# Two more tiles of attention in three rounded terms, and the last of the ring's tiles summed by a transfer

## The reference, cut to what matters

```python
kv = context @ Wkv;  k, v = split(kv);  q = layernorm(x) @ Wq       # B=8, N=56, M=1500, D=128, 16 heads of 64
dots = einsum('bhnd,bhmd->bhnm', q, k) * 64 ** -0.5
dots = dots - (1 - mask)[:, None, :, None] * 1e6
out = einsum('bhnm,bhmd->bhnd', softmax(dots), v)                    # heads merged
x = x + out @ Wout + bout
h = gelu(einsum('etd,edf->etf', layernorm(x).reshape(8, T, D), w1) + b1)   # one expert for each batch, F=512
x = x + (einsum('etf,efd->etd', h, w2) + b2).reshape(x.shape)
```

## Time and profile before

| | |
|---|---|
| median of 3 runs | 373.58 us (373.33 to 374.76) |
| the profiled execution | 373.79 us, of it span 371.9 us from the first to the last instruction |
| TensorE clock granted | 0.998 of full speed over the span |
| TensorE, VectorE, ScalarE, GpSimd busy | 97%, 75%, 68%, 31% of the span |
| scores, line 444 | 576 matmuls of 448 columns |
| float32 tiles, line 484 | 248 records; split tiles, line 477: 192 |
| exponential, seed, ex_hi (ScalarE) | 917, 911, 937 ns each |
| ex_lo, addition, half copy of shift_row (VectorE) | 1088, 1090, 620 ns each |

### The profile page before, as it was taken

How to read it: one execution, slowest core, us unless ns; L and a number is a source line. 1 busy time by engine, 2 the same in 40 slices (tenths; PEclk the granted TensorE clock), 3 DMA queues, 4 the chain that set the end, 5 groups by cost and what they waited for, 6 DMA issues and landing times.

```text
span 371.9 us, 5778 instructions
## 1 busy us (share of the span) xinstructions
PE 361.5 (97%) x1713; PEld 277.4 (75%) x1713; DVE 278.7 (75%) x458; ACT 254.6 (68%) x335; POOL 114.8 (31%) x125
## 2 busy tenths in 40 slices
PE   7899999999999999999999999999999999999994
PEld 7667777777877877777777877777777877677754
DVE  5888667877787778978797669978697669454863
ACT  3456577697669566797769576797579476896621
POOL 1610573145313530145314430254314440022000
PEclk9999999999999999999999999999999999999999
DMA  7696369328942846339932854349933752338400
GB/s 238 215 187 179 62 118 208 88 84 151 202 112 75 158 81 152 84 95 235 235 99 82 148 99 132 84 114 234 227 87 95 136 99 49 119 71 153 74 2 6
DMA packets 30622, 47.10 MB, mean 127 GB/s; under 512 B 2011, under 2 KB 21371, under 8 KB 30608
## 3 DMA queue, kind: packets, MB, share of 16 engines
q0 software_dynamic: 9936, 27.40, 37.8%
q1 hardware_dynamic: 20672, 19.52, 17.7%
HBM read 24.59 MB, written 0.23 MB: 67 GB/s over the span
## 4 chain that ended last, share of the span: by engine, by line
PE 88%; DVE 7%; DMA 2%; issue 2%; ACT 1%; SPq 1%; DVEq 0%; ACTq 0%
PE ps_s L444 30%; PE ps_a L484 24%; PE ps_x L500 11%; PE ps_a L477 10%; PE ps_x L533 3%; PE ps_a L421 2%; DVE ex_sum L901 2%; DMA ctxt_raw<-in_ctx_t 2%; PE ps_x L553 2%; PE ps_x L562 1%; PE ps_x L458 1%; PE ps_x L530 1%; PE ps_x L509 1%; PE ps_x L510 1%; DVE chunk_max L920 1%
## 5 line engine op out<-in xcount | busy, mean ns | idle before, releaser
L920 DVE TENSOR_REDUCE chunk_max<-ps_x 128x1 f32<-128x500 f32 x168 | 110.8, 677 | 29.3 <-PE ps_x L500 26.4
L709 ACT ACTIVATE ex_all<-ps_s 125x896 f32<-125x896 f32 x95 | 87.1, 917 | 39.0 <-PE ps_s L444 37.9
L484 PE MATMUL ps_a<-ex_all,ctx_sb 125*128 125x448 f32 x248 | 109.8, 540 | 0.0
L727 ACT COPY ps_s<-shift_row 125x896 f32<-125x896 f32 x94 | 85.7, 911 | 15.1 <-DVE shift_row L1058 12.6
L500 PE MATMUL ps_x<-ctxt_hi,qk_hi 128*128 128x500 f32 x168 | 80.0, 478 | 1.7 <-DVE chunk_max L920 1.2
L1236 POOL DMA_DIRECT2D ex_all<-ex_all x48 | 42.2, 878 | 115.3 <-ACT ex_all L709 110.9
L444 PE MATMUL ps_s<-qk_hi,ctxt_hi 128*125 128x448 f32 x192 | 73.9, 466 | 0.0
L484 PEld LDWEIGHTS ps_a<-ex_all,ctx_sb 125*128 125x128 f32 x248 | 46.2, 189 | 18.9 <-issue 14.6
L444 PE MATMUL ps_s<-qk_hi,ctxt_lo 128*125 128x448 f32 x192 | 54.9, 367 | 0.0
L444 PE MATMUL ps_s<-qk_lo,ctxt_hi 128*125 128x448 f32 x192 | 54.7, 366 | 0.0
L444 PEld LDWEIGHTS ps_s<-qk_hi,ctxt_hi 128*125 128x125 f32 x192 | 35.7, 187 | 22.3 <-issue 20.7
(11 more groups left out here) (110 smaller groups left out, 382.1 us busy)
## 6 DMA issues: line engine op xcount, KB each, us to landing
ex_all<-ex_all POOLq DMA_DIRECT2D x48, 448.0 KB, 4.6
ctxt_raw<-in_ctx_t SPq DMA_DIRECT2D x8, 750.0 KB, 6.8
ctx_sb<-in_ctx SPq DMA_DIRECT2D x8, 750.0 KB
ctxt_hi<-in_ctx_t POOLq DMA_DIRECT2D x21, 250.0 KB, 3.4
...
```

The costliest lines, as they stand in the source:

```text
L484: mm = nc.tensor.matmul(ps_a[:, c, 0:CH], ctx_sb[0:MT, u, t, :], ex(t)[0:MT, c * CH:(c + 1) * CH], start=(slot == 0), stop=(slot == TM - 1))
L709: nc.scalar.activation(half(ex(t)[0:MT, :]), src, ACT.Exp, scale=SCALE).then_inc(ex_ready, 1)
L727: nc.scalar.copy(ps_s[0:MT, t % 2, :, 0:CH], half(shift_row[0:MT, b.parity, :])).then_inc(seeded, 1)
L920: nc.vector.tensor_reduce(chunk_max[:, k, t:t + 1], filled()[:, 0:MC], AX.X, ALU.max).then_inc(job_free, 1)
```

## The change

- Tiles 7 and 9 are split too: `SPLIT` is 2, 4, 6, 7, 8, 9, in the last batch without 9. The order of the products is 6, 7, 8, 9 instead of 7, 6, 9, 8. `ctx_hi` and `ctx_lo` are made in two parts, the part of tiles 7 to 9 at t = 11 (ScalarE) and t = 4 (GpSimd).
- Tile 9 is added by a transfer into tile 0, except in the last batch. The additions left are 1 + 10, 2, 0, 11: two at (11, 0), one at (11, 1), one at (0, 0) of the next batch. The exponential of the next tile 0 now waits for the third of them.
- The seed of the next batch's tile 0 is copied from `ps_x` itself by ScalarE, which then copies `ps_x` into `shift_row` too and frees both jobs (`first_seed`); VectorE's two copies are gone, except for batch 0's.
- `sum_hi` shares the memory of `shift_diag`.

```diff
@@ -115,11 +115,13 @@
...
-    SUM_PARTS = [9, 1, 10, 2, 11]
-    SUMS = len(SUM_PARTS)
-    SPLIT = [2, 4, 6, 8]
-    PV_ORDER = [0, 1, 2, 3, 5, 4, 7, 6, 9, 8, 10, 11]
-    SPLITS, CTX_HI_AT = len(SPLIT), 5
+    CHAIN_TILES = [[3, 6, 9], [4, 7], [5, 8]]
+    SUM_PARTS, LAST_SUM_PARTS = [1, 10, 2, 0, 11], [0, 9, 1, 10, 2, 11]
+    SUMS, LAST_SUMS = len(SUM_PARTS) - 1, len(LAST_SUM_PARTS) - 1
+    SPLIT = [2, 4, 6, 7, 8, 9]
+    PV_ORDER = [0, 1, 2, 3, 5, 4, 6, 7, 8, 9, 10, 11]
+    SPLITS, CTX_HI_AT = len(SPLIT), (5, 11)
+    CTX_PARTS = [slice(0, 3), slice(3, 6)]
@@ -143,8 +145,8 @@
...
-    ADD_AT = {(10, 2): (0,), (11, 0): (1, 2)}
-    ADD_LATE = (3, 4)
+    ADD_AT = {(11, 0): (0, 1), (11, 1): (2,)}
+    ADD_LATE = (3,)
@@ -183,7 +185,7 @@
...
-        sum_hi = sb("sum_hi", [P, Q], F32R)
+        sum_hi = shift_diag[:, :, :].rearrange("p t q -> p (t q)")
@@ -268,22 +271,32 @@
...
+        def split(b):
+
+            return SPLIT[:-1] if b.off == B - 1 else SPLIT
+
+        def buffer_free(n):
+
+            return read_by(SPLIT[n - 2]) if n >= 2 else read_by(SPLIT[SPLITS - 2 + n]) - TM
...
         def summed(t):
-            return 1 + (SUM_PARTS.index(t) if t else 0)
+            return max(SUM_PARTS.index(t), 1)
...
         def added_by_dma(eng, b, t):
-            adds = LAST_DMA // CHAINS
-            eng.wait_ge(ex_added[t % CHAINS], b.at(16 * adds, 16 * (t // CHAINS)))
+            c, n = t % CHAINS, CHAIN_TILES[t % CHAINS].index(t)
+            eng.wait_ge(ex_added[c], b.at(16 * len(CHAIN_TILES[c]), 16 * (n + 1)))
@@ -564,7 +577,8 @@
...
             def shift_jobs():
-                for c in range(2):
+                for _ in range(2):
+                    c = jobs.n % 2
                     shift_rows(job()[:, 0:CH], P, c, start=True).then_inc(job_ready, 1)
@@ -712,19 +726,25 @@
...
-                if n >= 2:
-                    act.wait_ge(pv_done, b.at(TM, read_by(SPLIT[n - 2])))
+                wait(act, pv_done, b.at(TM, buffer_free(n)))
                 nc.scalar.copy(ex_hi[0:MT, n % 2, :], ex(t)[0:MT, :]).then_inc(ex_hi_ready, 1)
...
+            def first_seed(b):
+
+                act.wait_ge(job_ready, jobs.value())
+                act.wait_ge(ex_ready, b.at(TM, -1))
+                nc.scalar.copy(ps_s[0:MT, 0, :, 0:CH], ps_x[0:MT, :, 0:CH]).then_inc(seeded, 1)
+                nc.scalar.copy(half(shift_row[:, b.parity, :]), ps_x[:, :, 0:CH]).then_inc(job_free, 2)
@@ -806,15 +826,18 @@
                     elif prepare:
                         if t + 2 == TM:
                             jobs.n = FIRST_JOBS if first else jobs.n + 2
+                            first_seed(b.later(1))
+                        else:
                             act.wait_ge(job_free, jobs.value())
-                        seed(b.later(1), t + 2 - TM)
+                            seed(b.later(1), 1)
...
+                        for part in range(2):
+                            ctx_high_part(b, part)
+                    if t in CTX_HI_AT and prepare:
+                        ctx_high_part(b.later(1), CTX_HI_AT.index(t))
+                    if t in split(b):
                         ex_high_part(b, SPLIT.index(t))
                     if pair is not None and t == GELU_AT[0]:
                         gelu_sigmoid(pair)
@@ -888,21 +911,20 @@
...
-                t = SUM_PARTS[n]
+                parts, by_dma = (LAST_SUM_PARTS, LAST_DMA) if b.off == B - 1 else (SUM_PARTS, TM)
                 dst = ex_sum[0:MT, b.parity, :]
-                left = ex(0)[0:MT, :] if n == 0 else dst
-                if n == 0:
-                    added_by_dma(dve, b, LAST_DMA - CHAINS + 1)
-                if t < CHAINS:
-                    added_by_dma(dve, b, LAST_DMA - CHAINS + 1 + t)
-                else:
-                    dve.wait_ge(ex_ready, b.at(TM, t + 1))
+                left = ex(parts[0])[0:MT, :] if n == 0 else dst
+                for t in parts[0:2] if n == 0 else parts[n + 1:n + 2]:
+                    if t < CHAINS:
+                        added_by_dma(dve, b, max(s for s in CHAIN_TILES[t] if s <= by_dma))
+                    else:
+                        dve.wait_ge(ex_ready, b.at(TM, t + 1))
                 wait(dve, ex_summed, b.at(SUMS, n))
                 nc.vector.tensor_tensor(dst, left, ex(t)[0:MT, :], ALU.add).then_inc(ex_summed, 1)
@@ -1068,7 +1090,7 @@
...
                     if prepare and at == SHIFT_AT:
-                        shift_copies(b.later(1))
+                        jobs.n += 2
@@ -1113,7 +1135,7 @@
...
-                    if (at[0] - 1, at[1]) in [(t, 1) for t in SPLIT]:
+                    if (at[0] - 1, at[1]) in [(t, 1) for t in split(b)]:
                         ex_low_part(b, SPLIT.index(at[0] - 1))
@@ -1235,18 +1257,19 @@
...
+            def ctx_low_part(b, part):
...
-                    if CHAINS < t <= LAST_DMA + 1:
+                        ctx_low_part(b, 0)
+                    if CHAINS < t <= LAST_DMA + (2 if prepare else 1):
                         add_by_dma(b, t - 1)
@@ -1259,11 +1282,15 @@
...
+                    if t == 4:
+
+                        pool.wait_ge(ex_lo_ready, b.at(SPLITS, 1))
+                        ctx_low_part(b, 1)
...
                         pool.wait_ge(ex_lo_ready, b.at(SPLITS, 2))
                         ctxt_lo_chunk(b.later(1), 1)
-                        ctx_low_part(b.later(1))
+                        ctx_low_part(b.later(1), 0)
...
```

More of the change, by code:

```diff
@@ L253, in xattn_ffn @@
         ex_hi_ready, ex_lo_ready = sem("ex_hi_ready"), sem("ex_lo_ready")
-        ctx_hi_ready, ctx_lo_ready = sem("ctx_hi_ready"), sem("ctx_lo_ready")
+        ctx_hi_ready = [sem("ctx_hi_even_tiles"), sem("ctx_hi_late_tiles")]
+        ctx_lo_ready = [sem("ctx_lo_even_tiles"), sem("ctx_lo_late_tiles")]
         ex_summed, pv_done, att_ready = sem("ex_summed"), sem("pv_done"), sem("att_ready")
@@ L514, in last_sum_job @@
                 bank = job()
-                pe.wait_ge(ex_summed, b.at(SUMS, SUMS + c))
+                pe.wait_ge(ex_summed, b.at(SUMS, LAST_SUMS + c))
                 nc.tensor.matmul(bank[:, 0:CH], ones[0:MT, :], ex_sum[0:MT, b.parity, c * CH:(c + 1) * CH],
@@ L698, in exponentials @@
                     wait(act, pv_done, b.at(TM, read_by(before) - TM))
-                    if before > LAST_DMA:
+                    if before in SUM_PARTS:
                         wait(act, ex_summed, b.at(SUMS, summed(before) - SUMS))
@@ L714, in ex_high_part, with ctx_high_part @@
                 act.wait_ge(ex_ready, b.at(TM, t + 1))
-                if n >= 2:
-                    act.wait_ge(pv_done, b.at(TM, read_by(SPLIT[n - 2])))
+                wait(act, pv_done, b.at(TM, buffer_free(n)))
                 nc.scalar.copy(ex_hi[0:MT, n % 2, :], ex(t)[0:MT, :]).then_inc(ex_hi_ready, 1)
-            def ctx_high_part(b):
+            def ctx_high_part(b, part):
                 act.wait_ge(ctx_in[b.parity], b.at_every_other(16, 16))
-                nc.scalar.copy(ctx_hi[0:MT, b.parity, :, :], ctx_split(b)).then_inc(ctx_hi_ready, 1)
+                nc.scalar.copy(ctx_hi[0:MT, b.parity, CTX_PARTS[part], :], ctx_split(b, part)).then_inc(ctx_hi_ready[part], 1)
             def seed(b, t):
@@ L813, in iteration @@
                     if t == 1 and first:
-                        ctx_high_part(b)
-                    if t == CTX_HI_AT and prepare:
-                        ctx_high_part(b.later(1))
-                    if t in SPLIT:
+                        for part in range(2):
+                            ctx_high_part(b, part)
+                    if t in CTX_HI_AT and prepare:
+                        ctx_high_part(b.later(1), CTX_HI_AT.index(t))
+                    if t in split(b):
                         ex_high_part(b, SPLIT.index(t))
@@ L903, in add_last @@
             def add_last(b):
-                dve.wait_ge(ex_summed, b.at(SUMS, SUMS - 1))
+                dve.wait_ge(ex_summed, b.at(SUMS, LAST_SUMS - 1))
                 for c in range(2):
@@ L914, in ex_low_part @@
                 dve.wait_ge(ex_hi_ready, b.at(SPLITS, n + 1))
-                wait(dve, pv_done, b.at(TM, read_by(SPLIT[n - 2]) if n >= 2 else read_by(SPLIT[n - 2]) - TM))
+                wait(dve, pv_done, b.at(TM, buffer_free(n)))
                 nc.vector.tensor_tensor(ex_lo[0:MT, n % 2, :], ex(SPLIT[n])[0:MT, :], ex_hi[0:MT, n % 2, :].bitcast(F32),
@@ L1054, in shift_copies @@
             def shift_copies(b):
-                wait(dve, seeded, b.at(TM, -TM - 2))
-                for c in range(2):
+                for _ in range(2):
+                    c = jobs.n % 2
                     nc.vector.tensor_copy(shift_row[:, b.parity, c * CH:(c + 1) * CH], filled()[:, 0:CH]).then_inc(job_free, 1)
@@ L1236, in add_by_dma @@
                 pool.dma_start(ex(t % CHAINS), ex(t), accum_op=ALU.add).then_inc(ex_added[t % CHAINS], 16)
-            def ctx_low_part(b):
-                pool.wait_ge(ctx_hi_ready, b.at(1, 1))
```

(7 more changed lines are left out.)

10 lines of the change are left out of this document (5 added, 5 removed).

## The result

The changed kernel takes 376.49 us in the median of 4 runs (375.74 to 376.95), the kernel before 373.45 beside it. The ratio is 1.0069, with a 95% interval of 1.005 to 1.0087: slower by 0.7%. The profiled execution took 376.71 us with a span of 374.7; before it was 373.79 and 371.9, so the two traces stand 2.8 us apart in span.

The account below looks back on a forecast made before the run. TensorE was taken to bound the kernel's middle, where its cuts and new waits count in full. Saving -4.1, VectorE +3.9, landing +3.0 and last batch +0.3 gave +3.1 us: median 376.7, range 372.0 to 378.5.

Parts of the forecast that it names:

- The saving, 0.27 us a tile: TensorE, 15 tiles (7 and 9, in the last batch 7): three rounded terms replace two float32 halves, 4.1 us less.
- VectorE's stretch in the pair batches: Batches 2, 4, 6, hidden layer's drain to shift_diag: added ex_lo of tile 7 delays TensorE 1.3 us each, 3.9 in all.
- there, or on the way: Batch 4: TensorE loses 1.26 us at the shift matmuls or earlier, waiting some tenths for ex_lo of tile 7.
- over 1 us of idle time at the shift matmuls: Sign in batches 2, 4, 6: TensorE idles over 1 us there, released by shift_diag, with VectorE full.
- The late landing of tile 9: Ends of batches 1, 3, 5: landing (191.1 in batch 3) delays addition, qk_hi and TensorE's first maximum, 1.0 us each, 3.0 total.
- The choice between 4.2 and 8.4 us: Batch 3's transfers: a lone one's 4.2 us means no loss; tile 8's 8.4, followed by tile 9, was taken: 1.0 lost.
- ScalarE and GpSimd, 0: ScalarE's some 3 us more per batch and GpSimd's issue and split subtraction fit idle or waiting time: cost 0.
- Only VectorE: Rival, chance 0.27: only the VectorE stretch costs, tile 9 lands before 190.1; +0.1, 373.7 us.
- only the landing: Rival, chance 0.05: only tile 9's transfer landing costs, not VectorE's stretch; -0.8, 372.8 us.
- The saving lands: Rival, chance 0.11: neither VectorE's stretch nor tile 9's landing costs; 369.5 to 370 us.
- Slower still, by ScalarE: Rival, chance 0.07: TensorE also waits for seeds of tiles 1 to 3, some 0.4 us in 7 batches; 379.5 us.

Follow-up runs that it names:

- e1: Changed kernel, with ex_lo of tile 7 one place earlier on VectorE, ahead of the hidden layer's drain: 374.06 us, ratio 1.0016 to the kernel before.
- e5: Changed kernel, with ex_lo of tiles 7 and 9 earlier on VectorE and the output job at (11, 3): 373.29 us, ratio 0.9988 to the kernel before.
- e4: Changed kernel, with GpSimd's third ctxt_lo chunk at t = 10, so the 750 KB ctxt_raw load follows tile 9's transfer: 380.0 us, ratio 1.0182 to the kernel before.
- e6: Changed kernel, with tile 9 added by VectorE again instead of a transfer, additions in their old order: 372.93 us, ratio 0.9977 to the kernel before.
- e7: Changed kernel, with the edits of e5 and e6 together: 369.9 us, ratio 0.9908 to the kernel before.

## Why the prediction was right

It said 376.7 and slower, by one mechanism at two places, and both are there.

**The saving, 0.27 us a tile.** Right: the plain batches are shorter by 0.51 to 0.57, tile 9 takes 1.23. No wait for another engine shows there from tile 2 on.

**VectorE's stretch in the pair batches.** Right in place and kind. shift_diag was to end at 230.48 and ended at 230.42; no idle time stood before it; moving only ex_lo of tile 7 takes the batch from +0.7 to +0.1 (e1), and two more moves to -0.4 (e5). The term was 1.3 a batch and measured 1.24 (0.70 + 0.54). That TensorE loses half at tile 7 and half at the shift matmuls was named on record ("there, or on the way"); so its idle time at the shift is 0.33 us. The sign to look for, over 1 us of idle time at the shift matmuls, was put too sharply: the sum is right, the place half right.

**The late landing of tile 9.** Right: 190.7 against 191.1 on record, from the spacing of queued additions (here 2.2 us, 188.5 to 190.7). The choice between 4.2 and 8.4 us was what decided the forecast, and e4 shows its reason, the load ahead: without it the same transfers take 4.2 to 4.6. The loss of 1.0 measured 0.85 to 1.30 and follows the landings, 7.4 us in batch 1, 7.3 in 3 and 7.7 in 5. The Trainium skill, page "DMA: Bandwidth & Descriptors", section "Queues, rings and completion order", has descriptors taken in ring order on each DMA engine, in a paragraph on the queues of SyncE and ScalarE; these transfers are GpSimd's. The trace agrees with such an order for them: tile 9 lands 2.2 us behind tile 8 though issued 3.1 behind. In batch 0 the landing (5.3 us from 62.44) costs nothing, as forecast.

**ScalarE and GpSimd, 0.** Right for this kernel. The copy from PSUM to PSUM takes 0.89 us, the one to shift_row 0.92, against an assumed 0.91; no scores wait for a seed. But ScalarE's longer order was only hidden behind VectorE's stretch: with the stretch shorter, 0.42 us a pair batch came out (e1).

**What was off.** The seed from PSUM, with VectorE's two copies gone, was costed at nothing and is a gain: 0.36 us at the start of batch 1, and 0.2 at each of three others, where in the kernel after the landing covers it (e6 uncovers it). The last feed-forward was costed at nothing and lost 0.60, of it 0.55 to the half clock. The head ran 0.55 early. -0.36 - 0.55 + 0.60 nearly cancel, so that the total agrees so well (+2.8 in span, +3.0 in medians, +3.1 on record) is partly luck.

**The rivals.** "Only VectorE" and "only the landing" each fall, since e5 and e6 take away one of the two and leave the other whole. "The saving lands" had the price of 369.5 to 370 right, for another kernel: e7, with both causes gone, takes 369.9. Its profiled execution has the gain of the seeds in it, about 1.0, and the loss of the clock, 0.9, so the agreement is partly luck too. "Slower still, by ScalarE" has nothing for it in the kernel after.

**Left open.** Why the clock falls in the tail in one execution at 366.4 and in another at 370.4 or not at all before the end: among the four runs of the kernel after the time goes with the mean granted clock (375.74 at 1.0, 376.26 at 0.998, 376.71 at 0.995, 376.95 at 0.991), but among those of before it does so less clearly, and two long executions of e7 had a full or nearly full clock. I tried nothing on it. Open too is why the same transfer of tile 9 in batch 1 took 7.4 us in the kernel after and 6.3 in e1.
